# Attention stage: at most one maxima room per step, shared rooms, a longer lead-in, and key blocks added on VectorE

## The reference, cut to what matters

```python
scale = np.float32(1.0 / np.sqrt(D))                  # 16 heads of D = 32
att = jnp.einsum('bhqd,bhkd->bhqk', q, k) * scale     # layer 0: 1024 queries, 1024 keys
att = jnp.where(causal[None, None], att, -jnp.inf)
y = jnp.einsum('bhqk,bhkd->bhqd', jax.nn.softmax(att, axis=-1), v)
attc = jnp.einsum('bhqd,bhkd->bhqk', qc, kc) * scale  # layer 0: 1024 queries, 2048 context keys
y = y + jnp.einsum('bhqk,bhkd->bhqd', jax.nn.softmax(attc, axis=-1), vc)
...
attn = jax.nn.softmax(scores, axis=-1)                # layer 1: 1024 queries, 2048 context keys
out = jnp.einsum('bhqk,bhkd->bhqd', attn, vh)
```

## Time and profile before

| | |
|---|---|
| median of 3 runs | 4285.14 us |
| the profiled execution | 4297.94 us, span 4296.3 us, mean granted TensorE clock 0.918 |
| attn0, first to last scores | about 470 to 1650 us |
| attn1, first to last scores | about 2454 to 3298 us |
| PE, busy share of the span | 89% |
| VectorE, ScalarE, POOL | 59%, 47%, 42% |

### The profile page before, as it was taken

The page is one execution under the profiler, slowest core; times in us unless marked ns, Lnnn a source line. Parts: engine busy times, 40 slices in busy tenths (PEclk is TensorE's granted clock), DMA queues, the critical chain, the costliest instruction groups (busy, mean ns, idle before and its releaser), DMA issues. The chain is left out here.

```text
span 4296.3 us, 77223 instructions
## 1 busy us (share of the span) xinstructions
PE 3806.6 (89%) x30668; PEld 2654.1 (62%) x30668; DVE 2547.8 (59%) x3210; ACT 2019.5 (47%) x3511; POOL 1795.2 (42%) x878
## 2 busy tenths in 40 slices
PE   7989599999999998738997599999998739999997
PEld 5768355655655564427996455555554428888886
DVE  4345677777777774465664577777773464433342
ACT  2222265665666665006663266666664014443342
POOL 0000377777777777001110178888886000111110
PEclk9999699999999999759998799999999759999999
DMA  4478514423332430406663622222211323433331
GB/s 166 165 250 293 140 55 98 102 69 97 92 96 69 98 87 23 173 26 230 208 211 98 186 69 80 80 76 79 77 45 38 137 82 108 127 115 111 118 106 36
DMA packets 287914, 485.13 MB, mean 113 GB/s; under 512 B 22288, under 2 KB 117520, under 8 KB 285584
## 3 DMA queue, kind: packets, MB, share of 16 engines
q1 hardware_dynamic: 272016, 443.00, 33.9%
q0 software_dynamic: 14080, 37.76, 3.7%
q10 hardware_dynamic: 1536, 0.40, 0.0%
HBM read 350.67 MB, written 130.02 MB: 112 GB/s over the span
## 5 line engine op out<-in xcount | busy, mean ns | idle before, releaser
L833 DVE TENSOR_REDUCE attn_parts<-attn_mx 128x4 f32<-128x2048 f32 x540 | 1236.9, 2291 | 468.6 <-PE attn_mx L675 464.6
L789 ACT ACTIVATE attn_probs<-attn_low 128x512 f32<-128x512 f32 (+1 forms) x2368 | 1238.4, 595 | 553.4 <-PE attn_low L701 421.8
L656 POOL TENSOR_TENSOR attn_psums<-attn_psums,attn_probs 128x1024 f32<-128x1024 f32 x560 | 1330.7, 2376 | 84.9 <-ACT attn_probs L789 17.5
L701 PE MATMUL attn_low<-attn_queries,attn_keys 97*128 97x256 f32 (+1 forms) x4736 | 941.0, 318 | 22.5 <-DMA attn_queries<-attn_topT 16.5
L701 PEld LDWEIGHTS attn_low<-attn_queries,attn_keys 97*128 97x128 f32 x4736 | 680.2, 196 | 396.1 <-issue 200.5
L718 PE MATMUL attn_low<-attn_probs,attn_values 128*32 128x256 f32 x9472 | 657.1, 397 | 1.4 <-ACT attn_probs L789 1.4
L1451 DVE TENSOR_TENSOR ffn_wL<-ffn_raw,ffn_wH 128x2048 fp32r<-128x2048 f32 x128 | 293.5, 2293 | 223.4 <-ACT ffn_wH L1406 223.4
L1406 ACT ACTIVATE ffn_wH<-ffn_raw 128x2048 fp32r<-128x2048 f32 x128 | 245.3, 1916 | 338.3 <-DMA ffn_raw<-in_L_ffn_W_dram 177.4
L675 PE MATMUL attn_mx<-attn_keysn,attn_queriesn 32*128 32x512 f32 (+3 forms) x2400 | 311.9, 508 | 89.9 <-DVE attn_parts L833 45.7
L653 POOL TENSOR_TENSOR attn_psums<-attn_probs 128x1024 f32<-128x1024 f32 x88 | 209.5, 2380 | 424.9 <-ACT attn_probs L789 424.9
L718 PEld LDWEIGHTS attn_low<-attn_probs,attn_values 128*32 128x32 f32 x9472 | 253.2, 112 | 193.8 <-issue 20.9
(11 more groups left out here) (196 smaller groups left out, 4462.9 us busy)
## 6 DMA issues: line engine op xcount, KB each, us to landing
ffn_raw<-in_L_ffn_W_dram SPq DMA_DIRECT2D x128, 1024.0 KB, 5.5
attn_keys<-l_cross_keys SPq DMA_DIRECT2D x96, 512.0 KB, 5.5
attn_queries<-l_queries SPq DMA_DIRECT2D x48, 512.0 KB, 4.6
l_cross_keys<-projc_high SPq DMA_DIRECT2D x64, 256.0 KB
l_cross_keys<-projc_lowp SPq DMA_DIRECT2D x64, 256.0 KB
l_cross_values<-projc_vout SPq DMA_DIRECT2D x64, 256.0 KB
attn_keysn<-l_cross_keys SPq DMA_DIRECT2D x16, 1024.0 KB, 5.1
attn_values<-l_cross_values SPq DMA_DIRECT2D x32, 512.0 KB, 6.0
```

The lines of the kernel that those rows point to most:

```text
L656: pool.tensor_tensor(ps, ps, at, ALU.add).then_inc(added, 1)
L701: mm = pe.matmul(out[:, n0:], KS[b][0:3 * HD + 1, h, kb * P:(kb + 1) * P], QS[b][0:3 * HD + 1, h, job.qb * QB + n0:(job.qb + 1) * QB], sta ...
L789: act.activation(probs[:, m % RING, i // 2, heads, n0:], sc[:, item % SC, :].rearrange("p (h q) -> p h q", q=QB)[:, :, n0:], ACT.Exp, scal ...
L833: dve.tensor_reduce(parts[j % ROWS_DEEP][:, :, t, part], room[:, :, 0:cols], AX.X, ALU.max).then_inc(max_read, 1)
```

## The change

Groups: the last, narrow parts of an even causal job's two query blocks (128 and 256 columns) become one group in one room; each later step takes at most `max(need, 1)` groups; the lead grows from 8 to 11 groups, with the turns of finished jobs inside it. The masked operations write back into PSUM instead of to `fenced`. Sums: a causal job pools on POOL blocks 0, 1, 2, 4 only (one more ones group on 768 keys, two more on 1024 keys). A context job pools 0 to 5, 8, 9, 10, 14; blocks 6+7 and 12+13 (steps 3 and 6) are added on VectorE into `pair`, two heads in iteration m and two in m+1, and PE does one ones group for each pair in the next step's values; blocks 11 and 15 keep their ones groups. Inversion pieces come 1, 2, 3 and 6 steps after a job's last step (before: 2, 3, 4, 5), the normalization 7 (before: 6).

```diff
...
+        tails = []
         for t in range(QB // P):
             n = (qb * (QB // P) + t + 1) * P if unit.causal else unit.keys
             self.parts = -(-n // BLK)
             for part in range(self.parts):
                 cols = min(BLK, n - part * BLK)
-                self.groups.append((t, part, cols, unit.causal and part == self.parts - 1))
+                if unit.causal and cols < BLK and qb % 2 == 0:
+                    tails.append((t, part, cols, True, sum(x[2] for x in tails)))
+                else:
+                    self.groups.append(((t, part, cols, unit.causal and part == self.parts - 1, 0),))
+        if tails:
+            self.groups.append(tuple(tails))
         whole = [kb for kb, n0, masked in self.blocks if not masked]
-        self.pooled = whole if unit.causal else [kb for kb in whole[:-3] if kb < 4 or kb == 7 or kb % 2 == 0]
+        if unit.causal:
+            self.pooled = [kb for kb in whole if kb < 2 or kb % 2 == 0]
+        else:
+            self.pooled = [kb for kb in whole[:-1] if kb < 6 or kb in (8, 9) or kb % 4 == 2 and kb > 6]
+        self.paired = () if unit.causal else tuple(s for s in range(self.steps - 1) if s % 3 == 0 and s)
 
...
-        while done < len(due) and due[done] <= 0:
+        lead = max(g - x for g, x in enumerate(due[:24]))
+        while done < lead:
             self.place(done, -1)
             done += 1
         for m in range(n):
...
-                j, g = self.groups[done]
-                cols += self.jobs[j].groups[g][2]
-                if need <= len(self.groups_at[m]) > 0 and cols > BLK:
-                    break
+            while done < len(due) and self.free(done, m) and len(self.groups_at[m]) < max(need, 1):
                 self.place(done, m)
                 done += 1
...
+    def pairs(self, m):
+
+        return sum(first + s < m for first, s in self.pair_steps)
+
+    def pair_at(self, m):
+
+        return 0 <= m < self.steps and m - self.jobs[self.job_of[m]].first in self.jobs[self.job_of[m]].paired
...
         fence = ph.sb("fence", [P, BLK])
-        fenced = ph.sb("fenced", [P, GH, BLK])
...
         sc, acc = low[:, 0:SC, :], low[:, SC, :].rearrange("p (a q) -> p a q", q=QB)
         LEADS = len(plan.groups_at[-1])
+        lead_turn = {j: min(plan.groups_before[j + 1] + 1, LEADS) for j in plan.turn_at[-1]}
+
+        def turned_before(k):
+
+            return len([j for j in plan.turn_at[-1] if lead_turn[j] <= k]) if k < LEADS else 0
...
+        FLAT, STACK, ROW = 2, 11, QB // P
+        PIECE_AT = (1, 2, 3, 6)
+        PIECES, LATE = len(PIECE_AT), PIECE_AT[-1] + 1
 
...
-                        rows_h = slice(h * HD, (h + 1) * HD)
-                        mm = pe.matmul(room[:, h, 0:cols], QN[b][rows_h, q0:q0 + P],
-                                       KN[b][rows_h, part * BLK:part * BLK + cols], start=True, stop=True)
+                    if room is low and turned_before(k):
+                        pe.wait_ge(exped, turned_before(k))
+                    for t, part, cols, masked, at in job.groups[g]:
+                        q0 = (job.qb * (QB // P) + t) * P
+                        for h in range(GH):
+                            rows_h = slice(h * HD, (h + 1) * HD)
+                            mm = pe.matmul(room[:, h, at:at + cols], QN[b][rows_h, q0:q0 + P],
+                                           KN[b][rows_h, part * BLK:part * BLK + cols], start=True, stop=True)
                     mm.then_inc(max_ready, 1)
 
...
+                    if j in plan.turn_at[-1] and lead_turn[j] // 2:
+                        pe.wait_ge(max_read, lead_turn[j] // 2 * 2)
...
                     for i, (kb, n0, _) in enumerate(here):
-                        if kb in job.pooled:
+                        if kb in job.pooled or kb // STEP in job.paired:
                             continue
                         for h in range(GH):
                             mm = pe.matmul(acc[h * HD:(h + 1) * HD, 1, n0:], c["onesf"][:, 0:HD],
                                            probs[:, m % RING, i, h, n0:], start=False, stop=False,
                                            skip_group_check=True)
+                    if m > job.first and plan.pair_at(m - 1):
+                        pe.wait_ge(paired, 2 * plan.pairs(m))
+                        for h in range(GH):
+                            mm = pe.matmul(acc[h * HD:(h + 1) * HD, 1, :], c["onesf"][:, 0:HD], pair[:, h, :],
+                                           start=False, stop=False, skip_group_check=True)
                     mm.then_inc(valued, 1)
                     if m == job.last:
                         if job.pooled:
...
                     maxima(k)
-                pe.wait_ge(max_read, LEADS)
-                for j in plan.turn_at[-1]:
-                    turn(j)
+                    for j in plan.turn_at[-1]:
+                        if lead_turn[j] == k + 1:
+                            turn(j)
+                pe.wait_ge(max_read, LEADS // 2 * 2)
...
+                        if plan.pair_at(m - RING):
+                            act.wait_ge(paired, 2 * plan.pairs(m - RING + 1))
                     act.wait_ge(scored, item + 1)
                     heads = slice(2 * (i % 2), 2 * (i % 2) + 2)
...
                     turned(j)
-                for j in plan.turn_at[-1]:
                     set_row(j)
                 for m in range(N_STEPS + 1):
...
-                    t, part, cols, masked = jobs[j].groups[g]
                     dve.wait_ge(max_ready, k + 1)
                     room = low if k < LEADS and k % 2 else mx
-                    if masked:
-                        if k:
-                            dve.wait_ge(max_read, k)
-                        for h in range(GH):
-                            op = dve.tensor_tensor_reduce(fenced[:, h, 0:cols], room[:, h, 0:cols], fence[:, BLK - cols:],
-                                                          1.0, LOW, ALU.add, ALU.max,
-                                                          parts[j % ROWS_DEEP][:, h, t, part:part + 1])
-                        op.then_inc(max_read, 1)
-                    else:
-                        dve.tensor_reduce(parts[j % ROWS_DEEP][:, :, t, part], room[:, :, 0:cols], AX.X, ALU.max
-                                          ).then_inc(max_read, 1)
+                    for t, part, cols, masked, at in jobs[j].groups[g]:
+                        seen = room[:, :, at:at + cols]
+                        into = parts[j % ROWS_DEEP][:, :, t, part]
+                        if masked:
+                            for h in range(GH):
+                                op = dve.tensor_tensor_reduce(seen[:, h, :], seen[:, h, :], fence[:, BLK - cols:], 1.0, LOW,
+                                                              ALU.add, ALU.max, into[:, h:h + 1])
+                        else:
+                            op = dve.tensor_reduce(into, seen, AX.X, ALU.max)
+                    op.then_inc(max_read, 1)
                     if g == len(jobs[j].groups) - 1:
                         dve.wait_ge(max_read, k + 1)
                         if j >= TOPS:
...
+                def add_pair(m, half):
+                    dve.wait_ge(exped, plan.item[m, 2 + half] + 1)
+                    before = plan.pairs(m)
+                    if half == 0 and before:
+                        first, s = plan.pair_steps[before - 1]
+                        dve.wait_ge(valued, first + s + 2)
+                    heads = slice(2 * half, 2 * half + 2)
+                    dve.tensor_tensor(pair[:, heads, :], probs[:, m % RING, 0, heads, :], probs[:, m % RING, 1, heads, :],
+                                      ALU.add).then_inc(paired, 1)
+
                 dve.memset(fence[:, 0:BLK - P], 0.0).then_inc(fence_set, 1)
                 dve.tensor_copy(fence[:, BLK - P:], c["maskq"][:, :].bitcast(F32)).then_inc(fence_set, 1)
                 dve.wait_ge(fence_set, 2)
...
                     if m < N_STEPS:
                         for k in plan.groups_at[m]:
                             reduce(k)
-                    for piece in range(PIECES):
-                        if 0 <= m - 2 - piece < N_STEPS and plan.ends(m - 2 - piece) is not None:
-                            invert(plan.ends(m - 2 - piece), piece)
+                    for half in range(2):
+                        if plan.pair_at(m - half):
+                            add_pair(m - half, half)
+                    for piece, wait in enumerate(PIECE_AT):
+                        if 0 <= m - wait < N_STEPS and plan.ends(m - wait) is not None:
+                            invert(plan.ends(m - wait), piece)
 
```

More of the change, by code:

```diff
@@ L432, in __init__ @@
         self.steps = n
+        self.pair_steps = [(x.first, s) for x in self.jobs for s in x.paired]
         self.job_of = [j for j, job in enumerate(self.jobs) for _ in range(job.steps)]
@@ L452, in __init__ @@
                 need = max(need, -(-k // (due[g] - m + 1)))
-            cols = 0
```

(25 more changed lines are left out.)

3 lines of the change are left out of this document (1 added, 2 removed).

## The result

The changed kernel takes **4379.41 us** (median of 4 runs, 4373.19 to 4384.02), the kernel before 4286.98 us beside it: ratio **1.0215 [1.0195, 1.0234]**, 92 us slower. The profiled execution of after has a span of 4371.6 us, that of before 4296.3 us. Two executions far off the others, one of e1 (7131 us) and one of the kernel before beside e9 to e12 (5447 us), were slow ones and are left out of the ratios.

What follows compares the result with a forecast made beforehand. PE was taken to set the pace of both stages, attn0 also losing time to waits and half clock; 4297.9 - 40 - 85 - 19 + 10 + 218 + 38 = 4420 us profiled, 4407 us on the median's scale, range 4120 to 4480.

Steps and rivals of the forecast that it cites:

- Term 6: Context jobs: VectorE additions wait for POOL's running addition and delay the next; 3.4 us a job, +218 us.
- Term 7: Half clock on PE behind the waits for VectorE's additions; 0.6 us a job, +38 us.
- Term 1: Context jobs: seven ones groups become five, steps of a job total 25.14 us, 0.62 us less; -40 us.
- room's loop: Maxima room: matmuls 0.56 us, then reduce 2.29 us before PE refills it; bounds a step without ones group at 2.90 us.
- Terms 2, 3 and 4: attn0's stalls -85 us, the lead-in of attn1 -7 and attn0 -12 us, causal ones groups +10 us.
- Term 4: Causal jobs: 24 more ones groups on PE at 0.43 us each; +10 us.
- term 2: attn0: waits for second groups, POOL's causal sums and masked reduces go, with most half clock behind them; -85 us.
- Term 5: Small or hidden parts: masked operations, turns and row DMAs with two steps of lead, POOL's earlier block 5; 0.
- additions pass: Rival: POOL doesn't hold VectorE off, each addition lasts 0.69 us and hides; 4151 us, chance 0.33.
- Near balance: Rival: halves meet POOL between operations more often, costing 1.7 to 2.1 us a job; 4260 to 4285 us, chance 0.10.
- POOL late: Rival: additions pass, but block 5's ring slot and the total hold PE 0.7 us a job; about 4196 us, chance 0.05.
- Signs named beforehand: Expected if additions wait: mean 1.5 us or more, POOL's above 2.38, attn1's clock below 1.00, two PE reduce waits a job.

Runs made afterwards that it cites:

- e1: The changed kernel with ones groups on PE again for blocks 6, 7, 12 and 13 of context jobs, no additions on VectorE; 4204.8 us, ratio 0.9796.
- e9: e6 with POOL's list of blocks in context jobs as in the kernel before; 4183.0 us, ratio 0.9750.
- e12: e6 with all whole blocks of causal jobs added by POOL, as before the change; 4187.2 us, ratio 0.9761.
- e7: e4 with the transpose of a job's maxima one step earlier; 4140.3 us, ratio 0.9650.
- e10: e5 with each VectorE addition written as a reduction over the two blocks, same sums from one input; 4197.4 us, ratio 0.9787.
- e5: The changed kernel with the transpose of a job's maxima one step earlier; 4340.1 us, ratio 1.0123.
- e6: e1 with the transpose of a job's maxima one step earlier; 4186.9 us, ratio 0.9762.
- e4: The changed kernel with POOL's additions in context jobs cut to 4 of 1024 columns, most of that sum left out; 4222.2 us, ratio 0.9836.
- e8: The changed kernel with POOL's additions in context jobs replaced by fills of an unread buffer, that sum left out; 4217.4 us, ratio 0.9836.
- e3: The changed kernel with each VectorE addition replaced by a one-input maximum over 512 columns, those sums left out; 4212.0 us, ratio 0.9812.

## Why the prediction was right

The forecast was 4407 us with 0.54 for slower; 4379 is 28 us below it, and it is slower by the mechanism forecast.

**Term 6, the additions wait.** Right in kind. I put a half's wait at 0 to 2.51 us and a job's loss at 3.4 us. Halves take 0.68 to 2.88 us, mean 1.67. With term 7 I had 4.0 us a job. In attn1 it is 28.98 - 25.09 = 3.9 us, but 0.7 of it (28.98 - 28.32) is the row, which leaves 3.2. In attn0, first maxima to last total, after takes 1243.5 us and e7 1138.8: 105 / 32 = 3.3 us a job, the row included. The whole is 4340 - 4140 = 200 us with the row in time, against 256 predicted; the two terms together were too large by 56 us.

**Term 7, the clock.** Right in kind: attn1 fell to 0.96 after waits that were never over 2.0 us, while in e10, with waits of at most 0.6 us, it stayed at 1.00. The rule that I had quoted from the Trainium skill ("TensorE: Matmul & The Clock Gate", "HAM oscillation — how this bites in real kernels"), by which such short waits would cost no clock, does not hold in these runs. e5, where PE waits for no row, has 0.96 too from 2600 to 3100 us, with waits of at most 1.9 us.

The traces of e5 and e7 also tell the two terms apart. Between the first and the last total of each stage, e5 is 97.5 + 100.2 = 198 us longer. PE's waits for VectorE there are 134.5 us in e5 and 8.0 in e7, so some 127 us are waits; what is left, about 71 us, goes with the granted clock, 0.97 and 0.95 in e5 against 1.00 and 1.00. That is 2.0 and 1.1 us a job where I had 3.4 and 0.6: term 6 was too large by about 90 us and term 7 too small by about 33, so one error hid a part of the other.

**Term 1, the ones groups,** -40 us: -47 (e7 against e6). The job of 25.14 us was 25.09. The room's loop of 2.90 us bounds a step without ones group as I had it. In e7 POOL is nearly idle as well, but PE waits for POOL only 0.8 us in all of e6, so that hides little.

**Terms 2, 3 and 4** were -94 us together. e1 is 83 below before with a row that is late, e6 104 with one that is not. The parts were attributed wrongly: the shared rooms, which I had put down for the 1.0 us waits only, also remove the double steps, and the placement rule with the lead-in is worth 24 us. No run takes the shared rooms away alone, so their share of the rest is not measured. The waits for masked reduces (7.3 us before) did not all go as I had it: they are 13.2 us in after and 4.4 in e6. Term 4 was +10 for the groups, with POOL's 13.9 us of waits on the other side in term 2; with the new placement only 4.4 us of those waits come back, and e12 shows no net gain either way.

**Term 5 is the step that failed.** I wrote that the turns and the DMAs of the rows keep two steps of lead, and costed them at nothing. The lead in steps was indeed the same. But I did not count SP's store among what moves, nor the load queued behind it; and two steps had become shorter. That costs 39 us in after, and 82 where the additions pass.

**Luck in the number.** The 39 us that term 5 left out stand against the 56 us that terms 6 and 7 had too much. With the row priced rightly the forecast would have been 4446 us, 67 above the measured time in place of 28.

**The rival "additions pass"** was priced at 4151 us. e4, which makes them pass, takes 4222: the price forgot the row. With the row in time it is 4140. So had they passed, the kernel would have been 1.6% faster than before, not 3.1.

**Near balance and POOL late.** ScalarE does wait for POOL now, 36.8 us in 700, so the ring's slot is a real wait; in e10, without the collision, it is still there (31.0 us in the same stretch) and PE doesn't feel it.

**Signs named beforehand.** Mean addition over 1.5 us: 1.67. POOL's additions above 2.38: 2.46. attn1's clock below 1.00: 0.96. No wait of 2.4 us in attn0 and none for POOL at a causal end: so. attn1's first three steps 15 us: 13.01 (maxima of step 0 at 2439.68, of step 3 at 2452.69), less than said. PE waits for the reduce twice a job: 37 times in 24 jobs, so three times in two jobs.

## What to carry to other kernels

Before work goes from TensorE to VectorE, count its SBUF inputs and look at what POOL does meanwhile: two inputs against a reading POOL operation cost here two and a half times the bare duration, and held POOL too; the same sum from one input, as a reduction over a strided view, cost 1.245 us each time and left POOL's operations as they were. When a change moves a store or a drain by a step, write down what is queued behind it on its DMA queue, and whether that now overtakes a small, urgent transfer. And price the pieces of a change apart: this one held 83 us of gain (e1) and 175 us of loss.

## What the runs showed of the hardware

- A two-input VectorE operation (512 columns, 0.68 us) waits for the end of the running POOL operation that reads SBUF although POOL's operations are back to back: it gets in between two of them and ends 0.55 to 0.56 us after the first of them, in all 198 cases of after. It lasted up to 2.88 us, mean 1.67.
- The wait goes both ways: POOL's normalization of 256 columns, 0.73 us alone, took 1.18 us on average in after from 2600 to 3100 us, 0.73 in e4, e8 and e10.
- A POOL fill of 2.45 us does not hold it off (e8, 0.68 us), nor does a POOL addition hold off a one-input VectorE reduction (e3, 0.68 us; e10, 1.23 to 1.27 us).
- VectorE's reduction in SBUF over a stride of 1024 columns costs about as much per column as the one over neighbours in PSUM: 1024 columns in 1.245 us, 2048 in 2.29.
- The small transfer of the row was there when PE read it 3.1 us after its issue, where it went out ahead of a load; with a load issued 0.48 us before it, it took 4.1 us in e1 and up to 5.2 us in e4.
- In attn1 from 2600 to 3100 us, PE waits of at most 1.9 us went with a granted clock of 0.96 (after and e5), waits of at most 0.6 us with 1.00 (e10).
